# A graph attention kernel in which the mask of some score tiles is added by DVE instead of by TensorE

## The reference

```
q, k, v = x @ W.T + b                                  # 8 heads of 32
scores  = q k^T / sqrt(32);  scores = where(adj + I > 0, scores, -inf)
out     = softmax(scores) v;  h = layernorm(x + out @ Wo.T + bo) * gamma + beta
feat    = h @ fc_w.T + fc_b;  logits = q_dot + k_dot^T + (1 - adj) * -1e9
y       = softmax(leaky_relu(logits)) feat + h
```

## Time and profile before

| | us |
|---|---|
| Three runs | 1141.26, 1138.78, 1134.08 |
| Median | 1138.78 |
| The profiled execution | 1139.43 |
| Its span, first to last instruction | 1137.7 |
| TensorE busy | 1039.8 (91%) |
| DVE busy | 741.8 (65%) |
| POOL busy | 723.9 (64%) |
| ScalarE busy | 622.3 (55%) |

### The profile page before, as it was taken

One profiled execution on the slowest core, in us unless ns is written; L12 is line 12 of the kernel. 1 busy time (PEld: TensorE's weight loads), 2 busy tenths in 40 slices (PEclk: granted clock), 3 DMA queues, 4 the chain that ended last, 5 costly groups with the idle time before them and its releaser, 6 DMA issues.

```text
span 1137.7 us, 17894 instructions
## 1 busy us (share of the span) xinstructions
PE 1039.8 (91%) x5896; PEld 653.8 (57%) x5896; DVE 741.8 (65%) x1959; ACT 622.3 (55%) x1178; POOL 723.9 (64%) x415
## 2 busy tenths in 40 slices
PE   4788899999999999999999999999999999999676
PEld 3444455656666565666656565666656566665354
DVE  4554767676766768676766767676676867675332
ACT  2144466574737556564746657473755656474623
POOL 3054686676776666686766667677666668677840
PEclk9798999999999999999999999999999999999967
DMA  5344545353434445353444534353444435334010
GB/s 139 84 103 103 140 103 140 81 134 99 132 101 100 137 104 124 99 135 99 127 113 103 140 83 132 100 133 99 101 137 104 120 102 135 100 80 114 1 56 18
DMA packets 90763, 121.01 MB, mean 106 GB/s; under 512 B 18480, under 2 KB 45616, under 8 KB 90672
## 3 DMA queue, kind: packets, MB, share of 16 engines
q1 hardware_dynamic: 90672, 119.87, 40.4%
HBM read 52.44 MB, written 8.39 MB: 53 GB/s over the span
## 4 chain that ended last, share of the span: by engine, by line
PE 62%; DVE 14%; ACT 11%; issue 6%; POOL 4%; SPq 2%; DMA 1%; ACTq 0%; DVEq 0%; POOLq 0%
PE shared L391 16%; PE shared L509 10%; PE st_bank L525 8%; PE st_bank L527 7%; PE o_bank L465 7%; PE sm_bank L535 7%; DVE recip L882 3%; ACT z L677 3%; DVE sm_bank L947 3%; ACT e L742 3%; POOL e_sum L1044 2%; DVE masks L937 2%; PE shared L498 2%; DVE qt_lo L865 2%; PE shared L484 2%
## 5 line engine op out<-in xcount | busy, mean ns | idle before, releaser
L742 ACT ACTIVATE e<-st_bank 128x512 f32<-128x512 f32 x512 | 309.1, 605 | 396.5 <-PE st_bank L527 394.2
L947 DVE CUSTOM_DVE_ANT_0 sm_bank<-sm_bank,masks 128x512 f32<-128x512 f32 x512 | 351.7, 695 | 239.3 <-PE sm_bank L535 237.4
L535 PE MATMUL sm_bank<-kt_hi,q_pad 128*128 128x512 f32 x512 | 299.0, 586 | 17.0 <-issue 6.0
L1044 POOL TENSOR_TENSOR e_sum<-e_sum,e 128x1024 f32<-128x1024 f32 x128 | 302.2, 2390 | 6.2 <-ACT e L742 5.0
L525 PE MATMUL st_bank<-q_stack,k_stack 97*128 97x512 f32 x512 | 237.1, 464 | 0.8 <-ACT e L742 0.8
L527 PE MATMUL st_bank<-mask_t,ident_b 128*128 128x512 bf16 x512 | 201.7, 394 | 0.0
L1044 POOL TENSOR_TENSOR e_sum<-e 128x1024 f32<-128x1024 f32 x64 | 152.1, 2387 | 10.6 <-PE shared L475 8.2
L525 PEld LDWEIGHTS st_bank<-q_stack,k_stack 97*128 97x128 f32 x512 | 97.4, 190 | 93.6 <-issue 53.7
L465 PE MATMUL o_bank<-e,v 128*32 128x512 f32 x1024 | 137.2, 608 | 1.3 <-ACT e L742 1.3
L509 PE MATMUL shared<-feat,z 128*128 128x256 f32 x512 | 128.3, 397 | 1.4 <-ACT z L689 1.4
L535 PEld LDWEIGHTS sm_bank<-kt_hi,q_pad 128*128 128x128 f32 x512 | 104.7, 205 | 23.2 <-issue 11.9
(11 more groups left out here) (126 smaller groups left out, 1830.8 us busy)
## 6 DMA issues: line engine op xcount, KB each, us to landing
adj_in<-in_adj SPq DMA_DIRECT2D x32, 1024.0 KB, 5.8
q_stack<-qt_hi SPq DMA_DIRECT2D x256, 64.0 KB, 2.0
k_stack<-kt_hi SPq DMA_DIRECT2D x256, 64.0 KB, 2.0
x_in<-in_x SPq DMA_DIRECT2D x16, 512.0 KB, 4.4
q_pad<-qt_hi SPq DMA_DIRECT2D x128, 64.0 KB, 2.0
q_stack<-qt_lo SPq DMA_DIRECT2D x128, 64.0 KB, 2.0
k_stack<-kt_lo SPq DMA_DIRECT2D x128, 64.0 KB, 2.0
h<-in_x SPq DMA_DIRECT2D x16, 512.0 KB, 3.8
```

The source lines that it names most:

```text
L535: nc.tensor.matmul(sm_bank[s % 2][:, :], q_pad[j // GH][:, j % GH, qt * P:(qt + 1) * P], kt_hi[j // GH][:, :], start=True, stop=True).then ...
L742: nc.scalar.activation(e[:, kt, i, :], st_bank[s % 2][:, :], ACT.Exp, scale=SCALE)\
L947: nc.vector.tensor_tensor_reduce(sm_bank[s % 2][:, :], sm_bank[s % 2][:, :], mask[nxt if off else par][:, qt * N:(qt + 1) * N], 1.0, LOWES ...
L1044: nc.gpsimd.tensor_tensor(e_sum[:, pair, :], a, b, ALU.add).then_inc(pool_done.sem, 1)
```

## The change

At steps 9 to 16 of an iteration the matmul with the identity is gone. The product of k and q ends its accumulation by itself and signals `st_done`. DVE waits for that signal (and for the turned mask), adds `mask_t` to the bank in place, and signals a new semaphore `st_masked`. ScalarE's exponential waits for that one instead of `st_done`. At the other 24 steps nothing is different. On DVE the addition of step s stands ahead of the maximum of step s and behind all that step s - 1 issued.

```
--- before.py
+++ after.py
@@ -42,6 +42,7 @@
 EPS = 1e-5
 LOWEST = -3.0e38
 STACK = 3 * DH
+DVE_MASKED = (9, 10, 11, 12, 13, 14, 15, 16)
 LEAD = 20
 
 FIRST, LAST = -1, NB + 1
@@ -205,6 +206,7 @@
         tiles = [(s, 0) for s in range(POS)]
         st_done = Signal(sem("st_done"), tiles)
         exp_done = Signal(sem("exp_done"), tiles)
+        st_masked = Signal(sem("st_masked"), [(s, 0) for s in DVE_MASKED])
         sm_tiles = [(s, maxima_tile(s)[0]) for s in range(POS)]
         sm_done = Signal(sem("sm_done"), sm_tiles)
         max_done = Signal(sem("max_done"), sm_tiles)
@@ -522,10 +524,14 @@
                             pe.wait_ge(max_placed[i].sem, max_placed[i].after(f"g{g}", t if g else t - 1))
                         pe.wait_ge(exp_done.sem, exp_done.after((s - 2) % POS, t if s >= 2 else t - 1))
                         bank = st_bank[s % 2]
-                        nc.tensor.matmul(bank[:, :], k_stack[g][:, i, kt * P:(kt + 1) * P], q_stack[g][:, i, :],
-                                         start=True, stop=False)
-                        nc.tensor.matmul(bank[:, :], ident_b[:, :], mask_t[par][:, kt, :],
-                                         start=False, stop=True).then_inc(st_done.sem, 1)
+                        if s in DVE_MASKED:
+                            nc.tensor.matmul(bank[:, :], k_stack[g][:, i, kt * P:(kt + 1) * P], q_stack[g][:, i, :],
+                                             start=True, stop=True).then_inc(st_done.sem, 1)
+                        else:
+                            nc.tensor.matmul(bank[:, :], k_stack[g][:, i, kt * P:(kt + 1) * P], q_stack[g][:, i, :],
+                                             start=True, stop=False)
+                            nc.tensor.matmul(bank[:, :], ident_b[:, :], mask_t[par][:, kt, :],
+                                             start=False, stop=True).then_inc(st_done.sem, 1)
                     off, j, qt = maxima_tile(s)
                     if on(t, off):
                         if j % GH == 0 and qt == 0:
@@ -727,7 +733,10 @@
                 for s in range(POS):
                     g, kt, i = s // (POS // 2), s // GH % NT, s % GH
                     if on(t, 0):
-                        act.wait_ge(st_done.sem, st_done.after(s, t))
+                        if s in DVE_MASKED:
+                            act.wait_ge(st_masked.sem, st_masked.after(s, t))
+                        else:
+                            act.wait_ge(st_done.sem, st_done.after(s, t))
                         if i == 0:
                             n = max(kt, 1)
                             if g == 1:
@@ -939,6 +948,12 @@
                     last.then_inc(done, 1)
 
                 for s in range(POS):
+                    if s in DVE_MASKED and on(t, 0):
+                        kt = s // GH % NT
+                        dve.wait_ge(act_done.sem, act_done.after("mt1", t - 1))
+                        dve.wait_ge(st_done.sem, st_done.after(s, t))
+                        nc.vector.tensor_tensor(st_bank[s % 2][:, :], st_bank[s % 2][:, :], mask_t[par][:, kt, :], ALU.add)\
+                            .then_inc(st_masked.sem, 1)
                     off, j, qt = maxima_tile(s)
                     if on(t, off):
                         if off == 1 and j == 0 and qt == 0:
```

## The result

The changed kernel took **1123.84 us** (median of 4 runs, 1123.49 to 1125.77) against 1139.69 us for the kernel before in all its four runs (1134.08 to 1141.26). The ratio is 0.9869, with a 95% interval of 0.9848 to 0.9890: 1.3% faster. The forecast was 1127 us. The profiled execution took 1123.88 us, with a span of 1122.2 us against 1137.7 before.

The account below looks back on a forecast made before the run. TensorE was taken to bound the kernel, with DVE ending steps 9 to 18 after the change. 13 iterations x 1.1 us, + 0.3, - 2 x 0.95 give 12.7 us off 1139.4: 1127 us forecast, range 1116 to 1140 us.

Parts of the forecast that it names:

- A matmul is worth 0.233 us: On TensorE, each removed mask matmul saves a third of a step's 0.70 us; 128 of them at most 29.9 us.
- TensorE at steps 9, 10 and 11 saves 3 x 0.233 = 0.70 us: Before step 12, three removed mask matmuls let TensorE finish step 12's scores 0.70 us earlier less one step's 0.23.
- 13.31 us after 524.35: DVE works without a gap from step 12 to the end of q_lo at 537.66, gaining 1.15 us per iteration.
- TensorE idle ahead of m0: Ahead of the turned maximum at step 18, TensorE would wait about 0.7 us for DVE's q_lo.
- (a): ScalarE's o_hi and POOL's row of sums behind it start about 0.9 us later; about 1.8 us are left, no cost.
- (b): SP's row of stack DMAs and step 26's negated maximum move 0.86 us earlier, with over 1 us of cover: no cost.
- The edges: Iterations 1 and 15 each lose 0.95 us through o_hi and POOL's sums; iteration 0 gains 0.3 us at most.
- DVE keeping up: Rival at steps 9 to 18: TensorE alone holds the turned maximum, 1.87 us gained per iteration, 1117 us; chance 12%.
- No overlap: Rival on DVE: each addition holds it for its whole 0.69 us and a 0.04 us hop, 1134 us; chance 20%.
- The clock rival: TensorE's 0.7 us stop ahead of the turned maximum drops its clock to 1.2 GHz, slower at 1156 us; chance 8%.
- The gain given back by SP's chain: Rival: POOL's row or SP's chain later eats the gain and the edges lose, 1139 to 1141 us; chance 10%.
- The 0.233 us as a bubble: Case within the 10% rival of 1139 to 1141 us: removing matmuls does not shorten TensorE, as a bubble stays.

Follow-up runs that it names:

- the kernel without the mask: Against the kernel before, at steps 9 to 16 the mask is left out altogether, neither matmul nor addition, so it computes something else: 1119.70 us, median iteration 63.43 us.
- that with steps 9 to 11: Against the change, DVE adds the mask only at steps 9, 10 and 11, the other steps keep their matmul: 1136.20 us, iteration 64.56 us.
- the kernel with seven steps: Against the change, step 16's mask goes back to TensorE, so DVE adds at steps 9 to 15: 1126.24 us, median iteration 63.67 us.
- the kernel with the same eight steps and an early maximum 7: Against the change, DVE negates maximum 7 ahead of step 15's addition and maximum instead of behind them: 1122.48 us, median iteration 63.87 us.
- an instruction more in its row: Against the change, one more DVE tensor_tensor of two SBUF constants, which nobody reads, at step 14 of each iteration: 1143.96 us, median iteration 64.91 us.
- the kernel with step 21: Against the change, one more DVE tensor_tensor that nobody reads, behind the maximum of step 21, where DVE waits for TensorE: 1126.32 us, median iteration 63.87 us.
- with steps 12 to 16: Against the change, DVE adds the mask only at steps 12 to 16, steps 9 to 11 keep their matmul: 1133.46 us, median iteration 64.33 us.

## Why the prediction was right, and where it was off

- **A matmul is worth 0.233 us, not its 394 ns row.** Shown: seven of them are 1.61 us (1.63), seen in the kernel without the mask, two are 0.48 (0.47), in that with steps 9 to 11. The N/2.4 + 2.5 that the prediction took from the Trainium skill (TensorE: Matmul & The Clock Gate, Back-to-back issue gap) is given there for an isolated matmul; for a stream of weight loads and 512-column matmuls the same section has about 131 ns, with which these 0.233 us do not agree either.
- **"TensorE at steps 9, 10 and 11 saves 3 x 0.233 = 0.70 us"** failed for step 9, whose matmul saves nothing. Up to step 12 the change has won 0.49 us: past the first logits the scores of step 12 start at 524.78 - 495.25 = 29.53 us in the earlier trace rows and at 520.05 - 491.01 = 29.04 now. The copy of et ends last there. I had read step 9's products as work on the path, which they were, and not asked what would be late next.
- **"13.31 us after 524.35"**, DVE's gapless row, is 12.99 us, from addition 12 to the end of the low part of Q:

```profile
520.38 0.70 DVE L955 TENSOR_TENSOR st_bank<-st_bank,mask_t 128x512 f32<-128x512 f32 x1 [0.70 <-PE st_bank L528]
...
530.47 0.75 DVE L917 BATCH_NORM_STATS2 stats<-h 128x6 f32<-128x256 f32 x2
531.14 0.68 DVE L962 CUSTOM_DVE_ANT_0 sm_bank<-sm_bank,masks 128x512 f32<-128x512 f32 x1
...
532.62 0.75 DVE L874 SCALAR_TENSOR_TENSOR qt_lo<-shared,bias_col,qt_hi 128x512 fp32r<-128x512 f32 x1
```

  The additions are 0.59 to 0.61 us before the next start, as taken. The statistics take 0.67, not 0.77, and the aggregates 0.29, not 0.38: I had counted tails in full that overlap. This 0.3 us and step 9's 0.2 have opposite signs and nearly cancel. An ordinary iteration gains 1.19 us (65.04 to 63.85, the medians), and the mean gain is 1.15, the number of the walk, because one iteration of thirteen was 0.49 us longer over SP's row. So **that 1.15 us came out exactly is luck**; that it came out near is not. Then I used 1.1 and lost 13 x 0.05 = 0.65 us of it for nothing.
- **TensorE idle ahead of m0** for about 0.7 us: the last product of the projection starts at 532.52, m0 at 533.51, after 0.60 us marked as waiting, and the clock stays at 1.00:

```profile
532.52 0.40 PE L393 MATMUL shared<-xt_hi,weight_lo 128*128 128x512 f32 x1
533.51 0.27 PE L454 MATMUL shared<-ident,row_max 128*4 128x128 f32 x1 [0.60 <-DVE qt_lo L874]
```

- **(a) o_hi about 0.95 us later** within the iteration and no cost: 26.50 us past the first logits against 25.61, 0.89 later, and POOL's shift was in time.

```profile
517.51 0.61 ACT L722 CAST split_hi<-x_in 128x512 fp32r<-128x512 f32 x1
```

- **(b) SP's chain has "over 1 us of cover"** was wrong. The negated maximum of step 26 moved as forecast (57.90 us past the first logits instead of 58.74), but I looked at the maximum behind it and not at the key product that wants its bank. That starts 0.53 us behind its end:

```profile
548.91 0.28 DVE L883 TENSOR_SCALAR neg_max<-shared 4x128 fp32r<-4x128 f32 x1 [3.40 <-DMA q_stack<-neg_max]
```

```profile
549.72 0.40 PE L393 MATMUL shared<-split_hi,uk_hi 128*128 128x512 f32 x1
```

  Such cover, 0.11 to 0.83 us, was enough for the change in twelve of thirteen iterations; the kernel with seven steps had too little in four.
- **The edges.** Iteration 1 lost 1.62 us, not 0.95, and not through POOL: TensorE waits for exponential 9, and its clock stays at half for longer behind that. The 0.3 us of iteration 0 cannot be told from the scatter of the start. For iteration 15 the loss of 0.95 cannot be told at the end of the kernel. In the change POOL's shift comes 0.9 us later against the iteration's start, as forecast, but from the first logits of iteration 15 to the last product it takes 116.7 us instead of 118.6, and in the kernel with the same eight steps and an early maximum 7 it takes 119.6. 1.6 us of either difference are TensorE's clock in the last products (granted 0.70, 0.83 and 0.70), which take 10.21 us in that kernel; before and after:

```profile
1123.99 10.19 PE shared L509 x32
```

```profile
1110.03 8.58 PE shared L511 x32
```

  The other 1.2 us between the change and that last kernel lie ahead of those products, and these runs do not explain them. So of the 15.55 us between the two profiled executions, 14.95 are the 13 iterations', -1.62 is iteration 1's, and +0.34 ahead of it and +1.89 at the end are within what differs from one kernel to the next. The forecast's sum of 12.7 was 2.8 us short: 0.65 by 1.1 for 1.15, and 1.89 + 0.95 by the end, less 0.67 by iteration 1.
- **The rivals.** DVE keeping up (63.2 us an iteration) is out: an instruction more in its row is paid in full. No overlap is out by the distances of 0.59 to 0.61 us between starts of rows of 0.69; by these rows the additions do not behave as the Trainium skill has it (VectorE: DVE Perf Modes, The DRAIN you can't avoid), that the next one starts when the pipe is empty, though its page allows for earlier starts elsewhere. The clock rival is out within the iterations (1.00), and showed in small in iteration 1. The gain given back by SP's chain came true in part: in one iteration of the change, and in four of the kernel with seven steps. The 0.233 us as a bubble is out by the kernel without the mask, where seven of them arrive.
- **The chances** were set with the border of 1% at 1127.4 us. "Within 1%" had 0.48 and faster 0.42; the result of 1.3% is on the faster side, by those 2.8 us, of which the end's part is not the change's doing as far as these runs tell. The 1% that I took as what a measurement can tell was too wide: the interval of the result is 0.2% to either side.

## What to carry to other kernels

When work leaves the busiest engine, walk the chain again and ask at each removed piece what it had been covering: here a copy on ScalarE took back the first step's saving, DVE the last ones', and a bank's release behind a row of DMA issues made some iterations long. Put added work on the second engine only up to where its own gapless row starts to bound, and look there for instructions that others wait for (an early negation, cheap to move, went with no long iterations at seven or eight steps). Read a kernel's mean and median iteration apart: a bound without slack shows first as a few long iterations, not as a shift of all.

## What the runs showed of the hardware

- **The same DVE instruction takes 0.68 us or 1.11 us and more, by what POOL does.** The extra instruction reads two f32 tensors from SBUF. At step 21, where POOL stands idle (behind its `shift` at 534.72 it has nothing until 541.60), it took 0.675 us in each of the fourteen iterations between 154 and 987 us. At step 14, started while an addition of POOL was under way, it took 1.109 to 2.585 us, median 1.133. POOL at that time:

```profile
530.32 4.72 POOL L1062 TENSOR_TENSOR e_sum<-e_sum,e 128x1024 f32<-128x1024 f32 x2
```

  The Trainium skill (SBUF — State Buffer, section Who interferes with whom) says that a VectorE instruction with two SBUF inputs contends with a GpSimd one that reads SBUF, and one with at most one SBUF input, outside the two-port modes, does not. The durations agree, and their ends say more: in all sixteen iterations the instruction at step 14 ended 0.547 to 0.554 us behind the end of the POOL addition that it had met, however long that still took, and so did the one at step 21 in the last iteration (1.678 us, 0.547 behind). That is what standing still until POOL is done would give, and not a slower pace. In iteration 0 of the kernel with step 21, where POOL's addition had started only 0.17 us earlier, DVE took 0.675 us and POOL 3.09 instead of 2.4. The additions of this change, with one operand in PSUM, stayed at 0.69 us beside a busy POOL. That the port is the cause was not tried by itself. The longer duration also means that this experiment measured 1.1 us of DVE's time, not 0.6, and its expectation was missed for that reason.
- **About 3% of SP's issues in these rows take 1.0 to 2.2 us instead of 0.59**: 23 to 31 of 896 in every kernel here (24 before, 25 after). What makes them long stays open.
- **TensorE's clock in the drain** (two levels: a share near 0.50 of 2.4 GHz is 1.2 GHz) sets 8.6, 9.3 or 10.2 us for the same 32 last products: the granted clock over them was 0.83 in the change, 0.77 with steps 12 to 16 and 0.70 before, and length times clock is 7.1 to 7.2 us each time. The start differs by up to 5 us from kernel to kernel (the copy of v in iteration 0), and there the clock between 20 and 30 us does not go with it. So differences of 2 us between such kernels are better read from the iterations between than from the total.
